# Expert stage of a routed MLP: transposes by DMA in place of TensorE, second product two tiles behind

## Chip, cores and metric

One of the eight cores of a Trainium2 chip runs the kernel. The metric is device time in microseconds from one launch, median of several runs; the profile's span reaches from the first to the last instruction of one profiled execution.

## What is computed

The input x is 8 x 512 rows of 512. A cross-attention layer over 120 context rows is added to x, and then an MLP in which each row goes through one of eight experts.

```python
x = x + xattn(ctx, ctx, layernorm(x), Wk, Wv, bv, Wq, bq, Wo, bo)     # scores, softmax, values, Wo
xf = layernorm(x)
idx = argmax(softmax(xf @ Wg + bg))                                   # one expert of 8 per row
h = gelu(xf @ W1[idx] + b1[idx])                                      # 512 -> 512
x = x + h @ W2[idx] + b2[idx]                                         # 512 -> 512
```

## The kernel before

The first part of the span computes attention for 32 tiles of 128 rows, the gate, and for each row its expert. GpSimd scatters each row (512 values, minus the mean, the inverse deviation, the row's number) to a buffer in HBM that is sorted by expert. A small table is then made, on the chip, of NJ = 39 tiles of 128 rows, each of one expert: its start row in the buffer and the offsets of its weights and biases.

The expert stage, which the change touches, takes these 39 tiles in turn. All weights lie in SBUF as two f16 halves (a high part, and a low part scaled by 64), which VectorE and ScalarE made in the first part (L571, L774). Per tile j:

- SP reads the start row (`first_row`, L376) and loads 128 rows (`load_rows`, L381), 258 KB, into one of R = 3 row buffers. It waits for `res_ready`, so until GpSimd has read the buffer that it overwrites.
- GpSimd normalizes the rows to the f32 tile xn2 (`xhat`, L508), copies the row ids (L515), adds b2 and the rows into a buffer of its own (`residual`, L516), and scatters the finished tile to the output (`send`, L521), two tiles behind. `residual` waits for the landing of an earlier scatter from the same buffer.
- TensorE transposes xn2 in four blocks of 128x128 f32 into a bank of PSUM (L1246). ScalarE copies the bank to f16, the high half (L696), and VectorE subtracts it from the bank for the low half (L986).
- TensorE makes the first product, `up`: eight matmuls with the high half of the rows against both halves of the weights (L1254), then four with the low half (L1258). VectorE adds b1 (`bias`, L981), ScalarE applies gelu in f32 (L702).
- TensorE transposes the gelu (L1270), ScalarE and VectorE split it as above (L707, L991), and TensorE makes the second product, `down` (again L1254, L1258). VectorE adds it to the residual (`finish`, L997).

The order on each engine is written by hand. In TensorE's stream one step is:

```python
up(j, ex)
transpose_x2(j + 1)
down(j - 1, ex_before)
transpose_g(j)
```

Six such steps are one turn of a loop, at whose head TensorE loads seven weight offsets into registers (`experts`). Before the stage TensorE waits until all weights are split (`low_done`).

## Time and profile before

| | us |
|---|---|
| runs | 511.59, 511.91, 509.14 |
| median | 511.59 |
| span of the profiled execution | 495.3 |
| expert stage, first product to end of span | 257.8 |

The profiled execution's own time is not listed apart from the runs; the median is 16.3 us above its span. The stage's first product starts at 237.53 us.

How to read it: the page gives the busy time of each engine over the span, and the span in 40 slices of 12.4 us, in which each digit is a busy share in tenths. The expert stage begins in the twentieth slice. The chain of waits goes back from the last instruction to what released it, and so names what sets the end; its pieces carry start and length. The views by windows and by line give how much each engine has to do in a stretch and how long one instruction takes.

### The profile page before, as it was taken

To read this page: it belongs to the slowest core of one execution; us is meant where nothing else is said; L and a number is where in the kernel's file an instruction comes from. 1 tells how busy PE (TensorE), PEld (TensorE's weight loads), DVE (VectorE), ACT (ScalarE), POOL (GpSimd) and SP (SyncE) were. 2 spreads that over 40 slices of the span, in tenths; PEclk is the share of its full clock that TensorE was granted. 3 is DMA by queue.
4 is the path that set the end of the run, shared out by engine and by line. 5 is a ranking of instruction groups with operands and counts; after the bars stand their busy time and mean duration, and the time that the engine had idled before them with its cause. 6 is when DMAs were issued, how large, how long until landed. Compare 5 with 4: busy or idle time off the path is not lost.

```text
span 495.3 us, 9245 instructions
## 1 busy us (share of the span) xinstructions
PE 436.0 (88%) x2362; PEld 257.4 (52%) x2363; DVE 258.2 (52%) x604; ACT 200.7 (41%) x411; POOL 189.8 (38%) x274
## 2 busy tenths in 40 slices
PE   6758999997999999920699999999999999999991
PEld 2355565565777676610355555555555555555540
DVE  0246999674577677767244444444444444434440
ACT  1142366547788887652122222222222222222220
POOL 7000002300054545453245545545545545545530
PEclk9969999999999999975799999999999999999996
DMA  8999985905356555684522222322222222222200
GB/s 254 309 314 384 376 280 209 369 2 207 121 155 203 166 174 171 180 328 145 183 79 88 71 78 81 88 81 79 91 71 85 85 84 85 70 85 74 65 2 0
DMA packets 33850, 73.97 MB, mean 149 GB/s; under 512 B 4376, under 2 KB 4388, under 8 KB 33575
## 3 DMA queue, kind: packets, MB, share of 16 engines
q1 hardware_dynamic: 26591, 54.22, 34.5%
q0 software_dynamic: 6400, 19.23, 10.2%
q10 hardware_dynamic: 840, 0.29, 0.4%
q8 instruction: 9, 0.15, 0.1%
q14 instruction: 10, 0.08, 0.1%
HBM read 54.50 MB, written 21.06 MB: 153 GB/s over the span
## 4 chain that ended last, share of the span: by engine, by line
PE 81%; DMA 5%; DVE 3%; issue 3%; POOL 2%; SPq 1%; ACT 1%; POOLq 0%; DVEq 0%; ACTq 0%
PE bank L1254 28%; PE bank L1258 14%; PE bank L1198 5%; PE bank L1180 5%; DMA work<-in_ctx 5%; PE bank L1160 4%; PE bank L1110 4%; PE bank L1270 3%; PE bank L1246 3%; PE bank L1088 3%; PE bank L1173 3%; PE bank L1191 1%; PE bank L1070 1%; PE bank L1183 1%; PE bank L1139 1%
## 5 line engine op out<-in xcount | busy, mean ns | idle before, releaser
L1254 PE MATMUL bank<-expert_weights,work 128*128 x624 | 149.2, 382 | 7.5 <-issue 5.8
L1254 PEld LDWEIGHTS bank<-expert_weights,work 128*128 128x128 f16 x624 | 61.3, 98 | 66.2 <-issue 11.3
L1258 PE MATMUL bank<-expert_weights,work 128*128 x312 | 80.5, 381 | 0.0
L696 ACT ACTIVATE work<-bank 128x512 f16<-128x512 f32 x39 | 23.3, 597 | 102.6 <-PE bank L1246 102.6
L981 DVE SCALAR_TENSOR_TENSOR work<-bank,keys_then_b 128x512 f32<-128x512 f32 x39 | 27.0, 692 | 64.1 <-PE bank L1258 64.1
L571 ACT ACTIVATE expert_weights<-expert_weights 128x512 f16<-128x512 f32 (+1 forms) x64 | 38.7, 626 | 40.2 <-DVE expert_weights L774 39.4
L997 DVE SCALAR_TENSOR_TENSOR work<-bank,work 128x512 f32<-128x512 f32 x39 | 27.0, 692 | 52.9 <-PE bank L1258 52.9
L707 ACT ACTIVATE work<-bank 128x512 f16<-128x512 f32 x39 | 23.3, 597 | 69.7 <-PE bank L1270 69.7
L521 POOL DMA_INDIRECT out_x<-work,output_ids x39 | 40.1, 1028 | 26.5 <-DVE work L997 18.7
L1258 PEld LDWEIGHTS bank<-expert_weights,work 128*128 128x128 f16 x312 | 30.7, 98 | 37.5 <-issue 1.1
L516 POOL TENSOR_TENSOR work<-work,values_then_b 128x512 f32<-128x512 f32 x39 | 49.1, 1258 | 0.0
L473 POOL DMA_INDIRECT routed_rows<-work,slot_index x32 | 32.3, 1010 | 35.4 <-DVE slot_index L868 28.1
L515 POOL COPY output_ids<-work 128x1 int32<-128x1 int32 x39 | 6.9, 178 | 99.4 <-DMA out_x<-work,output_ids 89.4
L774 DVE SCALAR_TENSOR_TENSOR expert_weights<-expert_weights 128x512 f16<-128x512 f32 (+1 forms) x64 | 41.7, 686 | 1.6 <-ACT expert_weights L571 1.2
L744 DVE BATCH_NORM_STATS2 stats<-expert_weights 128x6 f32<-128x512 f32 x32 | 20.5, 682 | 32.8 <-DMA expert_weights<-in_x 32.8
L986 DVE TENSOR_TENSOR work<-bank,work 128x512 f16<-128x512 f32 x39 | 27.0, 692 | 17.8 <-ACT work L696 17.8
L1198 PE MATMUL bank<-values_then_b,work 120*128 (+1 forms) x64 | 35.3, 634 | 0.0
L1246 PE MATMUL bank<-identity,work 128*128 128x128 f32 x156 | 23.9, 277 | 11.5 <-POOL work L508 11.5
L1180 PE MATMUL bank<-keys_then_b,work 128*128 (+1 forms) x256 | 33.8, 275 | 0.0
L508 POOL TENSOR_SCALAR work<-work 128x512 f32<-128x512 f32 x39 | 29.6, 759 | 7.5 <-DMA work<-routed_rows 6.0
L991 DVE TENSOR_TENSOR work<-bank,work 128x512 f16<-128x512 f32 x39 | 27.0, 692 | 9.7 <-ACT work L707 9.7
L1180 PEld LDWEIGHTS bank<-keys_then_b,work 128*128 128x128 f32 x256 | 31.2, 192 | 0.5 <-issue 0.5
(154 smaller groups left out, 613.6 us busy)
## 6 DMA issues: line engine op xcount, KB each, us to landing
expert_weights<-in_L_ffn_W SPq DMA_DIRECT2D x14, 1024.0 KB, 9.3
work<-routed_rows SPq DMA_DIRECT2D x39, 258.0 KB, 2.7
expert_weights<-in_x SPq DMA_DIRECT2D x16, 512.0 KB, 8.7
expert_weights<-in_x SPq DMA_DIRECT2D x32, 256.0 KB, 3.0
routed_rows<-values_then_b POOLq DMA_DIRECT2D x9, 258.0 KB, 9.3
expert_weights<-in_L_ffn_W SPq DMA_DIRECT2D x8, 256.0 KB, 3.1
keys_then_b<-in_L_ffn_b SPq DMA_DIRECT2D x1, 2048.0 KB, 7.8
values_then_b<-in_L_ffn_b SPq DMA_DIRECT2D x1, 2048.0 KB, 10.5
```

Of the source, the lines that this page charges most:

```text
L473: pool.indirect_dma_start(routed, bass.IndirectOffsetOnAxis(ap=slot_i[:, j:j + 1], axis=0), rows[:, j, :], None).then_inc(sent[j], 16)
L508: nc.gpsimd.tensor_scalar(xn2, rrow[r][:, 0:D], rrow[r][:, D:D + 1], rrow[r][:, D + 1:D + 2], ALU.add, ALU.mult).then_inc(xn2_ready, 1)
L516: nc.gpsimd.tensor_tensor(res[r], rrow[r][:, 0:D], vals[:, bass.ds(ex, D)], ALU.add).then_inc(res_ready, 1)
L521: pool.indirect_dma_start(out_rows, bass.IndirectOffsetOnAxis(ap=out_id[:, r:r + 1], axis=0), res[r], None, bounds_check=T - 1, oob_is_err ...
L571: nc.scalar.activation(w_split[:, bass.ds(n * 2 * D, D)], wall[:, bass.ds((n + GAP) * D, D)], ACT.Copy, scale=WSCALE).then_inc(high_done, 1)
L774: nc.vector.scalar_tensor_tensor(w_split[:, bass.ds(n * 2 * D + D, D)], wall[:, bass.ds((n + GAP) * D, D)], WSCALE, w_split[:, bass.ds(n * ...
L981: nc.vector.scalar_tensor_tensor(hid, bank[1][:, :], 1.0 / WSCALE, keys[:, bass.ds(ex, D)], ALU.mult, ALU.add).then_inc(hb_done, 1)
L1180: mm(bank[2 + j % 2][:, 0:P], xnT[j % 2][:, c, :], keys[:, bass.ds((b * C + c) * P, P)], start=(c == 0), stop=False)
L1198: mm(bank[6 + j % 2][:, :], probT[j % 2], vals[0:K, bass.ds(b * D, D)], start=True, stop=True)\
L1246: last = nc.tensor.transpose(bank[0][:, P * c:P * (c + 1)], xn2[:, P * c:P * (c + 1)], ident[:, :])
L1254: mm(o, a[:, 0, c, :], w_split[:, bass.ds(first + (2 * c + h) * D, D)], start=(c == 0 and h == 0), stop=False)
L1258: last = mm(o, a[:, 1, c, :], w_split[:, bass.ds(first + 2 * c * D, D)], start=False, stop=(c == C - 1))
```

## The change

It takes all transposes of the expert stage from TensorE. xn2 and the gelu are split into f16 halves in their natural layout, by ScalarE and VectorE from SBUF; the two halves of a tile stand side by side, 128 rows of 1024 f16, and one DMA transpose, issued by SP, brings them into eight blocks of 128x128 for the products. There are two such DMAs in a tile, each with two buffers in turn.

The second product of a tile now comes two tiles behind its first. GpSimd adds b2 and VectorE adds the product in place in the row buffer, from which the scatter goes out; there are eight row buffers, and SP loads a tile four ahead once the scatter of eight tiles before has landed. SP starts with the transposes after all weights are split. All engines step through the tiles in loops of eight, and TensorE loads ten weight offsets per turn.

```diff
-R = 3
-NJTURN = NJ // R
+R = 8
+LAG = 2
+FIRST = 3
+NJTURN = (NJ - FIRST) // R
...
         rrow = [carve(ROW) for _ in range(R)]
-        res = [carve(D) for _ in range(R)]
-        xn2, x2T, hid, gel, gelT = (carve(D) for _ in range(5))
-        ge = carve(NJ * E).rearrange("p (j e) -> p j e", j=NJ)
-        tv = carve(4 * NJ).rearrange("p (v j) -> p v j", v=4)
+        xn2, hid, g0, g1 = (carve(D) for _ in range(4))
         assert at[0] <= U * ROW + 4 * D
-
-        x2T = x2T.bitcast(F16).rearrange("p (h c t) -> p h c t", h=2, c=C)
-        gelT = gelT.bitcast(F16).rearrange("p (h c t) -> p h c t", h=2, c=C)
-        out_id = sb("output_ids", [P, R], I32)
-
+        gel_split = [g.bitcast(F16) for g in (g0, g1)]
+        xn2_split = [split_area[:, n, :] for n in range(2)]
+        x2T = [w_split[:, E * NW * 2 * D + 2 * D * n:E * NW * 2 * D + 2 * D * (n + 1)].rearrange("p (k t) -> p k t", t=P)
+               for n in range(2)]
+        gelT = [bias_area[:, D * n:D * (n + 1)].bitcast(F16).rearrange("p (k t) -> p k t", t=P) for n in range(2)]
+        ge = g1[:, 0:NJ * E].rearrange("p (j e) -> p j e", j=NJ)
+        tv = g1[:, NJ * E:NJ * E + 4 * NJ].rearrange("p (v j) -> p v j", v=4)
...
+        def each_step(eng, step, first, end):
+
+            for n in range(first, FIRST):
+                step(Slot(n))
...
-            def load_rows(j, r, start):
-
-                sp.wait_ge(res_ready, j + 1)
-                sp.dma_start(rrow[r], routed[bass.ds(start, P), :]).then_inc(row_in[r], 16)
-
-            starts = [first_row(r) for r in range(R)]
+            def load_rows(t, start):
+
+                wait_apart(sp, out_sent[t.buf], 16 * t.turn, sp_waits)
+                sp.dma_start(rrow[t.buf], routed[bass.ds(start, P), :]).then_inc(row_in[t.buf], 16)
+
+            starts = [first_row(n) for n in range(3)]
...
+            sp.wait_ge(tabled, 3)
+            for n in range(3):
+                load_rows(Slot(n), starts[n])
...
-            with sp.Fori(1, NJTURN) as i:
-                for r in range(R):
-                    load_rows(i * R + r, r, first_row(i * R + r))
+            sp.wait_ge(low_done, E * NW)
+
+            def transpose_x2(t):
+                wait_apart(sp, x2l_done, t.j + 1, sp_waits)
+                wait_apart(sp, h_done, t.j - 1, sp_waits)
+                sp.dma_start_transpose(x2T[t.half], xn2_split[t.half]).then_inc(x2T_in[t.half], 16)
+
+            def transpose_g(t):
+                wait_apart(sp, gl_done, t.j + 1, sp_waits)
+                wait_apart(sp, y_done, t.j - 1, sp_waits)
+                sp.dma_start_transpose(gelT[t.half], gel_split[t.half]).then_inc(gT_in[t.half], 16)
+
+            def step(t):
+                if (t + 1).real:
+                    transpose_x2(t + 1)
+                if (t + 4).real:
+                    load_rows(t + 4, first_row((t + 4).j))
+                if (t - 1).real:
+                    transpose_g(t - 1)
+
+            each_step(sp, step, -1, NJ + 1)
...
+            def xhat(t):
+                wait_apart(pool, row_in[t.buf], 16 * t.turn + 16, pool_waits)
+
+                wait_apart(pool, x2l_done, t.j, pool_waits)
+                nc.gpsimd.tensor_scalar(xn2, rrow[t.buf][:, 0:D], rrow[t.buf][:, D:D + 1], rrow[t.buf][:, D + 1:D + 2],
                                         ALU.add, ALU.mult).then_inc(xn2_ready, 1)
...
+            def residual(t):
+
+                ex = pool.value_load(table[0:1, 2, bass.ds(t.j, 1)], min_val=0, max_val=(E - 1) * D)
+                nc.gpsimd.tensor_tensor(rrow[t.buf][:, 0:D], rrow[t.buf][:, 0:D], vals[:, bass.ds(ex, D)],
                                         ALU.add).then_inc(res_ready, 1)
 
-            def send(j, r):
-                wait_apart(pool, out_done, j + 1, pool_waits)
-                pool.indirect_dma_start(out_rows, bass.IndirectOffsetOnAxis(ap=out_id[:, r:r + 1], axis=0),
-                                        res[r], None, bounds_check=T - 1, oob_is_err=False).then_inc(out_sent[r], 16)
-
-            xhat(0, 0, 0)
-            xhat(1, 1, 0)
+            def send(t):
+                wait_apart(pool, out_done, t.j + 1, pool_waits)
+                ids_of = bass.IndirectOffsetOnAxis(ap=rrow[t.buf][:, D + 2:D + 3].bitcast(I32), axis=0)
+                pool.indirect_dma_start(out_rows, ids_of, rrow[t.buf][:, 0:D], None, bounds_check=T - 1,
+                                        oob_is_err=False).then_inc(out_sent[t.buf], 16)
...
+            def step(t):
+                if (t + 2).real:
+                    xhat(t + 2)
+                if t.real:
+                    residual(t)
+                if (t - 3).real:
+                    send(t - 3)
+
+            each_step(pool, step, 0, NJ + 3)
...
+            def x2_high(t):
+                act.wait_ge(xn2_ready, t.j + 1)
+                need(act, x2T_in[t.half], 16 * t.pair)
+                nc.scalar.activation(xn2_split[t.half][:, 0:D], xn2, ACT.Copy).then_inc(x2h_done, 1)
+
+            def gelu(t):
+                act.wait_ge(hb_done, t.j + 1)
+                nc.scalar.activation(hid, hid, ACT.Gelu).then_inc(g_done, 1)
+
+            def g_high(t):
+                act.wait_ge(g_done, t.j + 1)
+                need(act, gT_in[t.half], 16 * t.pair)
+                nc.scalar.activation(gel_split[t.half][:, 0:D], hid, ACT.Copy).then_inc(gh_done, 1)
+
+            def step(t):
+                if (t + 2).real:
+                    x2_high(t + 2)
+                if t.real:
+                    gelu(t)
+                    g_high(t)
+
+            each_step(act, step, -2, NJ)
...
+            def bias(t):
+                ex = dve.value_load(table[0:1, 2, bass.ds(t.j, 1)], min_val=0, max_val=(E - 1) * D)
+                dve.wait_ge(h_done, t.j + 1)
+                need(dve, gl_done, t.j)
+                nc.vector.scalar_tensor_tensor(hid, bank[t.half][:, :], 1.0 / WSCALE, keys[:, bass.ds(ex, D)], ALU.mult,
                                                ALU.add).then_inc(hb_done, 1)
 
-            def x2T_low(j):
-                dve.wait_ge(x2h_done, j + 1)
-                nc.vector.tensor_tensor(x2T[:, 1, :, :], bank[0][:, :].rearrange("p (c t) -> p c t", c=C),
-                                        x2T[:, 0, :, :], ALU.subtract).then_inc(x2l_done, 1)
-
-            def gT_low(j):
-                dve.wait_ge(gh_done, j + 1)
-                nc.vector.tensor_tensor(gelT[:, 1, :, :], bank[2][:, :].rearrange("p (c t) -> p c t", c=C),
-                                        gelT[:, 0, :, :], ALU.subtract).then_inc(gl_done, 1)
-
-            def finish(j, r):
-                dve.wait_ge(y_done, j + 1)
-                dve.wait_ge(res_ready, j + 1 + R)
-                nc.vector.scalar_tensor_tensor(res[r], bank[3][:, :], 1.0 / WSCALE, res[r], ALU.mult,
-                                               ALU.add).then_inc(out_done, 1)
-
-            def step(j, r):
-                if not isinstance(j, int) or j + 1 < NJ:
-                    bias(j + 1)
-                if not isinstance(j, int) or j + 2 < NJ:
-                    x2T_low(j + 2)
-                finish(j, r)
-                if not isinstance(j, int) or j + 1 < NJ:
-                    gT_low(j + 1)
-
-            x2T_low(0)
-            bias(0)
-            x2T_low(1)
-            gT_low(0)
-            with dve.Fori(0, NJTURN - 1) as i:
-                for r in range(R):
-                    step(i * R + r, r)
-            for r in range(R):
-                step(NJ - R + r, r)
+            def x2_low(t):
+                dve.wait_ge(x2h_done, t.j + 1)
+                nc.vector.tensor_tensor(xn2_split[t.half][:, D:2 * D], xn2, xn2_split[t.half][:, 0:D],
+                                        ALU.subtract).then_inc(x2l_done, 1)
+
+            def g_low(t):
+                dve.wait_ge(gh_done, t.j + 1)
+                nc.vector.tensor_tensor(gel_split[t.half][:, D:2 * D], hid, gel_split[t.half][:, 0:D],
+                                        ALU.subtract).then_inc(gl_done, 1)
+
+            def finish(t):
+                dve.wait_ge(y_done, t.j + 1)
+                dve.wait_ge(res_ready, t.j + 1)
+                nc.vector.scalar_tensor_tensor(rrow[t.buf][:, 0:D], bank[2 + t.half][:, :], 1.0 / WSCALE,
+                                               rrow[t.buf][:, 0:D], ALU.mult, ALU.add).then_inc(out_done, 1)
+
+            def step(t):
+                if (t - 3).real:
+                    finish(t - 3)
+                if (t - 1).real:
+                    g_low(t - 1)
+                if (t + 2).real:
+                    x2_low(t + 2)
+                if t.real:
+                    bias(t)
+
+            each_step(dve, step, -2, NJ + 3)
...
-            def product(o, a, first, low_ready, j):
-
+            def product(o, a, first):
 
                 for c in range(C):
                     for h in range(2):
-                        mm(o, a[:, 0, c, :], w_split[:, bass.ds(first + (2 * c + h) * D, D)],
+                        mm(o, a[:, c, :], w_split[:, bass.ds(first + (2 * c + h) * D, D)],
                            start=(c == 0 and h == 0), stop=False)
-                pe.wait_ge(low_ready, j + 1)
                 for c in range(C):
-                    last = mm(o, a[:, 1, c, :], w_split[:, bass.ds(first + 2 * c * D, D)], start=False, stop=(c == C - 1))
+                    last = mm(o, a[:, C + c, :], w_split[:, bass.ds(first + 2 * c * D, D)], start=False, stop=(c == C - 1))
...
+            def up(t, ex):
+                pe.wait_ge(x2T_in[t.half], 16 * t.pair + 16)
+                need(pe, hb_done, t.j - 1)
+                product(bank[t.half][:, :], x2T[t.half], ex).then_inc(h_done, 1)
+
+            def down(t, ex):
+                pe.wait_ge(gT_in[t.half], 16 * t.pair + 16)
+                need(pe, out_done, t.j - 1)
+                product(bank[2 + t.half][:, :], gelT[t.half], ex + C * 2 * D).then_inc(y_done, 1)
...
+            def steps(first, n):
+                ex = experts(first.j, n + LAG)
+                for q in range(n):
+                    t = first + LAG + q
+                    if t.real:
+                        up(t, ex[q + LAG])
+                    down(t - LAG, ex[q])
+
+            ex = experts(0, LAG)
+            for n in range(LAG):
+                up(Slot(n), ex[n])
+            steps(Slot(0), FIRST - LAG)
+            with pe.Fori(0, NJTURN) as i:
+                steps(Slot(FIRST - LAG, i), R)
+            last = FIRST - LAG + R * NJTURN
+            steps(Slot(last), NJ - LAG - last)
+            ex = experts(NJ - LAG, LAG)
+            for n in range(LAG):
+                down(Slot(NJ - LAG + n), ex[n])
```

## Rows read from the trace of the kernel before

**Rows 1.** the page: busy time, then tenths in 40 slices of clock and DMA

```profile
PE 436.0 (88%) x2362; PEld 257.4 (52%) x2363; DVE 258.2 (52%) x604; ACT 200.7 (41%) x411; POOL 189.8 (38%) x274
...
PEclk9969999999999999975799999999999999999996
DMA  8999985905356555684522222322222222222200
```

**Rows 2.** the chain of waits from 382 us: start us, us, what

```profile
382.18 0.44 PE bank L1270 x4
382.62 1.73 PE bank L1254 x8
384.34 0.86 PE bank L1258 x4
...
394.72 0.80 issue
395.53 1.90 PE bank L1254 x8
```

**Rows 3.** busy us of each engine in a window of six tiles

```profile
core 0: us, PE busy (x) PEld busy (x) DVE busy (x) ACT busy (x) POOL busy (x), PEclk, DMA share, GB/s
283.59:320.90 37.31, 36.50 (x193) 19.73 (x193) 16.54 (x25) 10.28 (x18) 19.10 (x25) 1.00 0.27 83
```

**Rows 4.** who waited for whom, 250 to 480 us: total, times, longest

```profile
POOL output_ids L515 <- DMA out_x<-work,output_ids: 89.4, 35, 2.7
```

**Rows 5.** by line, 250 to 480 us: line, engine, shapes, count, busy, mean ns

```profile
L516 POOL TENSOR_TENSOR work<-work,values_then_b 128x512 f32<-128x512 f32 x36 | 45.3, 1258 | 0.0
L521 POOL DMA_INDIRECT out_x<-work,output_ids x37 | 38.2, 1032 | 18.9 <-DVE work L997 11.1 <-issue 7.8
...
L508 POOL TENSOR_SCALAR work<-work 128x512 f32<-128x512 f32 x36 | 27.3, 758 | 0.8 <-DMA work<-routed_rows 0.8
...
L991 DVE TENSOR_TENSOR work<-bank,work 128x512 f16<-128x512 f32 x37 | 25.6, 692 | 9.1 <-ACT work L707 9.1
L702 ACT ACTIVATE work<-work 128x512 f32<-128x512 f32 x38 | 23.6, 622 | 2.8 <-DVE work L981 2.8
...
L707 ACT ACTIVATE work<-bank 128x512 f16<-128x512 f32 x37 | 22.1, 597 | 67.8 <-PE bank L1270 67.8
```

**Rows 6.** the page's groups that split weights out of SBUF

```profile
L571 ACT ACTIVATE expert_weights<-expert_weights 128x512 f16<-128x512 f32 (+1 forms) x64 | 38.7, 626 | 40.2 <-DVE expert_weights L774 39.4
...
L774 DVE SCALAR_TENSOR_TENSOR expert_weights<-expert_weights 128x512 f16<-128x512 f32 (+1 forms) x64 | 41.7, 686 | 1.6 <-ACT expert_weights L571 1.2
```

**Rows 7.** one line's instructions: SP's register load and row load; landing of the scatter

```profile
L376 SPq FUSED_REGOPS  x63: 37/152/170, 229.8 to 452.4; - x63
L376 SPq TENSOR_LOAD <-tile_table x39: 263/267/554, 229.3 to 452.1; - x39
...
L381 SPq DMA_DIRECT2D work<-routed_rows x39: 332/333/347, 231.9 to 457.7; - x39
...
DMA to landing us min/median/max: 2.5/2.7/4.4
...
DMA to landing us min/median/max: 2.1/2.8/2.9
```

**Rows 8.** the page: DMA queues

```profile
q1 hardware_dynamic: 26591, 54.22, 34.5%
...
q10 hardware_dynamic: 840, 0.29, 0.4%
```

**Rows 9.** the timeline at the stage's start: start us, us, instruction

```profile
234.50 0.76 POOL L508 TENSOR_SCALAR work<-work 128x512 f32<-128x512 f32 x1 [5.18 <-DMA work<-routed_rows]
...
237.53 3.59 PE L1254 MATMUL bank<-expert_weights,work 128*128 x8 [0.93 <-ACT work L696]
240.92 1.46 PE L1258 MATMUL bank<-expert_weights,work 128*128 x4
```

**Rows 10.** the chain of waits at the end: TensorE's last product

```profile
483.70 0.88 PE bank L1258 x4
```

158 lines of the change are left out of this document (46 added, 112 removed).

## The prediction

> **What bounds the kernel now.** [...] Eight matmuls take 1.73 us, the four with the low half 0.86 us, four transposes 0.44 us, and then the next product starts; the only break is 0.80 us of "issue" when the register loads for six tiles come [rows 2]. So one tile costs 2 x (1.73 + 0.86 + 0.44) = 6.06 us of TensorE, and the stage by its windows 37.31 us for six tiles, or 6.22 us with the register loads [rows 3]. No other engine comes near this: VectorE has 2.8 us of work in a tile, ScalarE 1.7 us, GpSimd 3.2 us, and GpSimd's waits are for the landing of its own scatter and end in time [rows 3 to 5]. TensorE is the bound, and 0.88 us of each 6.22 are transposes.
>
> **What is removed.** 2 x 4 transposes in each of 39 tiles: 39 x 0.88 = 34.3 us, all of it on the chain [rows 2]. A product without them costs 1.73 + 0.86 = 2.59 us, a tile 5.18 us. The register loads stay: 0.80 us before for seven values per six tiles; now ten values per eight tiles, between 0.80 and 0.80 x 10/7 = 1.14 us, so 1.0; 5.18 + 1.0/8 = 5.30 us per tile is the new floor. Also removed: the 0.18 us copy of row ids on GpSimd and its wait for the scatter (89.4 us in total), which cost nothing, since GpSimd was not late [rows 4].
>
> **What is only exchanged.** ScalarE's two copies to f16 now read SBUF instead of PSUM: 0.63 us in the nearest row, 0.60 before [rows 5, 6]. VectorE's two subtractions likewise: 0.69 in both [rows 5, 6]. These rows are both of whole 128x512 tiles, so the bounds are 0.03 us apart and TensorE hides them. VectorE keeps 4 x 0.69 = 2.8 us, ScalarE 0.62 + 2 x 0.63 = 1.9, GpSimd 0.76 + 1.26 + 1.03 = 3.05 us, all under 5.30 [rows 5, 6].
>
> **What is added: two DMA transposes per tile on SP.** Each moves 128 rows of 1024 f16, 256 KB, SBUF to SBUF; no row of the trace shows such an instruction. It has three prices.
>
> First, SP's own time, I. The lower bound is the plain issue of a transfer of the same size on the same engine, 0.33 us [rows 7]. That row cuts its transfer into 128 pieces; a transpose in blocks of 128 elements has 8 x 128 = 1024 pieces of 256 bytes. At the plain rate (0.33/128 = 2.6 ns a piece) that is 2.7 us; at the rate of GpSimd's scatter (1.03 us for 128 rows) it is 8.2 us [rows 5, 7]. I take 1.0 us, nearer to the plain row, because it is the same engine and a regular pattern; the range keeps the others. SP needs besides, in a tile, 0.33 us for the row load, and 0.27 + 0.15 us for its start row; with the waits I take 0.9 us [rows 7]. SP is hidden while 2I + 0.9 < 5.30, that is I < 2.2 us, and costs more than is gained from 2I + 0.9 > 6.22, I > 2.7 us.
>
> Second, the DMA engines. They are busy 27% of 37.31 us for six tiles, 1.68 us a tile for two transfers of 256 KB [rows 3]. With two more at that rate 3.4 us a tile: hidden. The hardware queue's mean packet costs 0.345 x 495.3 x 16 / 26591 = 103 ns for 2 KB, the small packets of queue 10 cost 38 ns for 345 bytes [rows 1, 8]; if each of 1024 pieces costs 38 ns, a transpose keeps the 16 engines 2.4 us and a tile 1.68 + 4.9 = 6.5 us. I take the lower one, since packet times hold latency that overlaps.
>
> Third, the latency, from issue to landing, L. Row loads land in 2.5 to 4.4 us, 2.7 in the median [rows 7]. I take 4.0 us for the transposes. The x half of tile t may start when the product of tile t-2 has let go of its buffer, and TensorE has three other products in between, 7.8 us. The gelu half: after the first product of t, VectorE's bias, gelu, copy, then on VectorE the finish of tile t-2 (which waits 2.6 us for its product), then the low half: done 4.1 us after the first product [rows 5, 6]. The second product of t comes four products after it, 10.4 us, so the transpose has 6.3 us. Both hide L = 4.0 us. That is what "two tiles behind" is worth: with one tile behind there would be 5.2 us for a chain of at least 2.9 + 2.7.
>
> **Added waits, and what is queued behind them.** On SP stands in order: x transpose of t+1, row load of t+4 (waits for the scatter of t-4, which lands 2.1 to 2.9 us after its issue), gelu transpose of t-1 [rows 7]. The scatter is issued 0.85 us after its product ends, so it has landed 3.7 us after that, or 1.1 us after the next first product is done; the gelu transpose behind it is due only 4.1 us after. Cost nothing; if the landing took 3 us more, the cover would be gone and TensorE would wait for the rest. On VectorE the bias of t is queued behind the low half of x of t+2; that waits for GpSimd, which is done a period earlier.
>
> **Start and end, by the timeline.** [...] After: copy 0.63, subtraction 0.69, L = 4.0, first product at 240.7, 3.2 us later, ending at 245.5 with the same 4.85 us. Tile 1 follows until 248.1. The transpose of tile 2 waits for the first product, lands at 249.5, its product ends 252.1; the gelu chain of tile 0 (2.8 us) with its transpose is ready at 252.3. So at 254.9 us four of 78 products are done. The other 74 x 2.59 = 191.7 and 7 register loads of 1.0 give 453.6. At the end the last gelu comes 8.1 us after the last first product, two products cover 5.2, so 2.9 us of stall: 456.5 us. Before, TensorE ends at 484.6 [rows 10]. What follows is the same, so 28.1 us are gained of the span of 495.3, to 467.2. The 16.3 us between the span and the median of 511.6 I leave as they are: **483.5 us**. With L = 2.7 start and end lose some 3 us less, 480; with a floor of 2.59 us per product and no stall, 477.
>
> [...] In rows, four transposes of 128x128 cost TensorE 0.44 us, 0.11 each, where they stand between products [rows 2]. [...]
>
> **Rival 1 (slower): SP's issue time becomes the period.** [...] It decides from I = 2.2 us, and is a loss above 2.7. For it: 1024 pieces instead of 128, and 2.7 us is just what the plain rate gives; SP also has all three DMAs of a tile in line. Against: the plain 256 KB issue is 0.33 us and SP is nearly empty now [rows 7]. At I = 3.5 us (an estimate between 2.7 and 8.2, in the lower part) a tile takes 7.9 us: 39 x (7.9 - 6.22) + 6 for start and end = 72 us more, 583 us. At I = 2.2 to 2.7 it lies between 484 and 518.
>
> [...]
>
> **Rival 2 (slower): the DMA engines become the period.** [...] From a transpose that takes 2.7 times as long as a plain transfer, 1.68 + 2 x 0.84 x 2.7 = 6.2 us, the gain is gone. At the 6.5 us worked out above: 39 x 0.3 + 6 = 18 us more, 529 us. For it: the price of small packets [rows 8]. Against: three quarters of the DMA time is free [rows 3].
>
> **Rival 3 (part of the gain).** A period between 5.5 and 6.0 us, because rate, latency and the order on SP act together: 490 to 507 us.
>
> **How the numbers follow.** Forecast (TensorE stays the bound, 477 to 490 us): 0.48. Rival 3: 0.07. Within 0.5%, which is about what a measurement of this kernel can tell from no change: 0.04, from the two slower rivals near their break-even. Rival 1 slower: 0.26. Rival 2 slower: 0.15. So faster 0.55, same 0.04, slower 0.41. The range has to hold both signs: from 475 (forecast without stalls, less the spread of the runs) to 600 (I = 3.7 us); left out are the dear ends of the rivals. If TensorE stays the bound, its own range is 477 to 490 us.
>
> **What the profile of the changed kernel will show.** Right: the chain in mid-stage is matmuls alone, windows of eight tiles take 42.4 us, the granted clock stays at the upper level, SP's transposes take under 2.2 us each, first product at about 240.7. Rival 1: TensorE waits for the transposes, SP's transposes fill the period back to back. Rival 2: SP idle or waiting, DMA share near its limit, landing times over 6 us. If TensorE has gaps in every tile, its clock may also fall to the lower level, as it is before the stage's first product [rows 1, 9], and a product would take twice the time, which would make either slower rival dearer. Wrong in all cases: if GpSimd or VectorE ends the wait of the matmuls.

## The result

The kernel after takes 483.12 us (median of 4 runs, 481.99 to 487.42), the kernel before beside it 511.75 us (509.14 to 513.35): ratio 0.9474, 95% interval 0.9434 to 0.9514, 28.6 us less. The forecast was 483.5 us, with 28.1 us less.

The profiled execution took 481.99 us and has a span of 480.3 us. So 1.7 us lie around the span, not 16.3: the profile that stands ahead of the prediction is of an execution some 15 us quicker than the median given with it. Where those microseconds lie is the first experiment's matter.

The page of after: busy time, the tenths of TensorE's clock and of the DMA engines, packets, and the hardware queue.

```profile
PE 409.1 (85%) x2050; PEld 223.8 (47%) x2051; DVE 251.8 (52%) x604; ACT 203.5 (42%) x411; POOL 188.7 (39%) x235
...
PEclk9969999999999988998557899999999999999997
DMA  7999975913535454458476999989888987999720
...
DMA packets 116221, 94.46 MB, mean 197 GB/s; under 512 B 86744, under 2 KB 86756, under 8 KB 115943
...
q1 hardware_dynamic: 108959, 74.68, 60.9%
```

Against [rows 1] TensorE is 27 us less busy, VectorE 6 us less; ScalarE and GpSimd are within 3 us of what they were. The DMA engines, at two tenths in the right half before, stand at eight and nine tenths. There are 116221 packets instead of 33850.

The chain of waits from the middle of the stage: start us, us, what.

```profile
338.89 1.73 PE bank L1292 x8
340.61 0.86 PE bank L1295 x4
...
356.15 0.86 PE bank L1295 x4
357.02 0.09 issue
357.11 1.90 PE bank L1292 x8
```

This is [rows 2] without its 0.44 us rows: a tile is 2 x (1.73 + 0.86) = 5.18 us, and at the loop head "issue" is 0.09 us instead of 0.80. A window of one loop turn, which is 8 tiles (window; busy us of PE, PEld, DVE, ACT, POOL; clock; DMA share; GB/s):

```profile
315.41:357.11 41.70, 41.61 (x193) 18.80 (x193) 20.35 (x33) 14.24 (x24) 25.40 (x24) 1.00 0.90 196
```

41.70 us for 8 tiles are 5.21 us a tile, where [rows 3] had 6.22. TensorE is still the bound, at the upper level of its clock (1.00 in this window). The DMA share is 0.90 instead of 0.27, that is 4.7 us of DMA time in a tile of 5.2. The transposes on SP, one line each for the x half and the gelu half (min/median/max ns), and the time from issue to landing of the gelu half and of the output scatter:

```profile
L450 SPq DMA_TRANSPOSE expert_weights<-key_bias_split_then_xn x39: 1231/1307/3336, 248.9 to 449.4; - x39
...
L455 SPq DMA_TRANSPOSE key_bias_then_geluT<-work x39: 746/1272/1599, 263.1 to 463.6; - x39
```

```profile
DMA to landing us min/median/max: 2.8/4.2/6.2
...
DMA to landing us min/median/max: 2.1/4.2/5.9
```

(The first landing row is of the same kernel in the run e5_after_again below.) A transpose keeps SP 1.3 us in the median, and that of the gelu half lands 4.2 us after its issue. The scatter's landing rose from 2.8 to 4.2 us [rows 7].

The start of the stage, by the chain of waits:

```profile
243.86 2.57 DMA work<-routed_rows
...
247.41 0.64 ACT key_bias_split_then_xn L754
...
248.17 0.70 DVE key_bias_split_then_xn L1039
...
248.94 6.94 DMA expert_weights<-key_bias_split_then_xn
...
256.01 1.03 PE bank L1292 x2
```

The first transpose needs 6.94 us to land. Ahead of it in the queue stands b2, 2 MB, issued at 245.31.

### The profile page after: what moved, and what is told of

It is laid out like the page before. It is cut to its first block, busy times and chain, and to the rows that moved or that the text cites. A ratio compares the mean times of both kernels' runs of the same rounds, so it can differ in the third digit from the quotient of the medians.

```text
span 480.3 us, 8534 instructions
## 1 busy us (share of the span) xinstructions
PE 409.1 (85%) x2050; PEld 223.8 (47%) x2051; DVE 251.8 (52%) x604; ACT 203.5 (42%) x411; POOL 188.7 (39%) x235
## 2 busy tenths in 40 slices
DMA packets 116221, 94.46 MB, mean 197 GB/s; under 512 B 86744, under 2 KB 86756, under 8 KB 115943
## 3 DMA queue, kind: packets, MB, share of 16 engines
q0 software_dynamic: 6400, 19.23, 11.1%
## 4 chain that ended last, share of the span: by engine, by line
PE 66%; DMA 11%; issue 5%; DVE 5%; SPq 4%; ACT 3%; POOL 2%; another core or an unknown queue 1%; ACTq 0%; DVEq 0%; POOLq 0%
PE bank L1292 24%; PE bank L1295 12%; DMA work<-in_ctx 5%; PE bank L1206 4%; PE bank L1226 4%; PE bank L1156 4%; PE bank L1244 4%; PE bank L1134 3%; PE bank L1219 3%; DMA key_bias_then_geluT<-work 3%; PE bank L1237 2%; PE bank L1116 1%; DMA expert_weights<-key_bias_split_then_xn 1%; ACT work L687 1%; SPq L450 1%
## 5 line engine op out<-in xcount | busy, mean ns | idle before, releaser
L1292 PE MATMUL bank<-expert_weights 128*128 x312 | 75.1, 384 | 22.2 <-DMA expert_weights<-key_bias_split_then_xn 20.8
L758 ACT ACTIVATE work<-work 128x512 f32<-128x512 f32 x39 | 24.6, 631 | 135.8 <-DVE work L1034 135.8
L589 POOL DMA_INDIRECT out_x<-work x39 | 45.3, 1162 | 87.2 <-DVE work L1050 85.0
L1292 PE MATMUL bank<-expert_weights,key_bias_then_geluT 128*128 x312 | 74.7, 383 | 4.5 <-DMA key_bias_then_geluT<-work 4.5
L1292 PEld LDWEIGHTS bank<-expert_weights 128*128 128x128 f16 x312 | 30.9, 99 | 60.8 <-issue 26.9
L1292 PEld LDWEIGHTS bank<-expert_weights,key_bias_then_geluT 128*128 128x128 f16 x312 | 30.7, 98 | 42.5 <-issue 7.7
L1295 PE MATMUL bank<-expert_weights,key_bias_then_geluT 128*128 x156 | 40.8, 385 | 0.0
L1295 PE MATMUL bank<-expert_weights 128*128 x156 | 40.0, 379 | 0.0
L1244 PE MATMUL bank<-values_then_b,work 120*128 (+1 forms) x64 | 37.3, 665 | 0.0
L797 DVE BATCH_NORM_STATS2 stats<-expert_weights 128x6 f32<-128x512 f32 x32 | 20.5, 682 | 31.5 <-DMA expert_weights<-in_x 31.4
L1226 PE MATMUL bank<-keys_then_b,work 128*128 (+1 forms) x256 | 35.1, 282 | 0.1
L1039 DVE TENSOR_TENSOR key_bias_split_then_xn<-work,key_bias_split_then_xn 128x512 f16<-128x512 f32 x39 | 27.0, 692 | 10.3 <-ACT key_bias_split_then_xn L754 10.3
L1044 DVE TENSOR_TENSOR work<-work 128x512 f16<-128x512 f32 x39 | 26.6, 682 | 2.7 <-ACT work L763 2.7
```

The costliest lines, as they stand in the source:

```text
L589: pool.indirect_dma_start(out_rows, ids_of, rrow[t.buf][:, 0:D], None, bounds_check=T - 1, oob_is_err=False).then_inc(out_sent[t.buf], 16)
L1039: nc.vector.tensor_tensor(xn2_split[t.half][:, D:2 * D], xn2, xn2_split[t.half][:, 0:D], ALU.subtract).then_inc(x2l_done, 1)
L1226: mm(bank[2 + j % 2][:, 0:P], xnT[j % 2][:, c, :], keys[:, bass.ds((b * C + c) * P, P)], start=(c == 0), stop=False)
L1244: mm(bank[6 + j % 2][:, :], probT[j % 2], vals[0:K, bass.ds(b * D, D)], start=True, stop=True)\
L1292: mm(o, a[:, c, :], w_split[:, bass.ds(first + (2 * c + h) * D, D)], start=(c == 0 and h == 0), stop=False)
L1295: last = mm(o, a[:, C + c, :], w_split[:, bass.ds(first + 2 * c * D, D)], start=False, stop=(c == C - 1))
```

## Experiments

The kernel before ran beside each of them: 498.83 us in the median beside e1 to e4, 499.30 beside e5 to e8, 499.74 beside e9 to e11, 12 to 13 us less than in the result above. Each ratio below is against the runs of before beside it. "After" means the changed kernel.

**1. The two kernels again (e1_before_again, e5_after_again).** No edit. The table of tiles was ready at 229.15 us in the profile of before and at 241.09 us in that of after, in a part that the change hardly touches. Either that is the change's doing and the stage gained 12 us more than it seems, or it belongs to the execution.

> The kernel before, unchanged, for a second profile. In the first profile of before the first product of the expert stage starts at 237.5 us and the span is 495.3; in that of after it starts at 256.0 us, of which some 12 us arose before the stage, in attention tiles whose code is the same. Theory A: these 12 us come and go with the program's execution and have nothing to do with the change; then this profile may show the first product near 249.5 us and a span of 507 to 510 us, which fits the timed runs of 509 to 513 us. Theory B: the change itself lengthened the first part; then 237.5 and 495 us again, and the timed runs of before stay 16 us above the span.

> The changed kernel, unchanged, beside the next three on one chip. Theory A (the 12 us by which its first profile was later before the expert stage belong to that chip, where before took 511.7 us too, and not to the change): on a chip where before takes 499 us the tile table is ready at 229 to 231 us, as in before, the first product starts at 244 to 246 us, and the ratio to before is 0.945 to 0.95 as in the first measurement. Theory B (the change itself lengthens the first part by 12 us): the table is ready at 241 us again and the ratio is 0.97.

Before: 499.76 us (498.25 to 502.19), table at 230.2 us. After: 471.77 us (469.65 to 472.04), table at 229.9 us, ratio 0.945 (0.9419 to 0.948). The first run alone decides nothing: its times lie at 499.8 us and not at 509 to 513, so what its two theories were to tell apart did not occur. The second does: table and ratio come as its theory A says. So the 12 us do not belong to the change. In the first measurement both kernels had them, here neither has them. Both kernels have 1.7 us around the span, so the prediction's "16.3 us around the span" was a slower attention part. In the first profile of after the delay arises between 145 and 218 us. Its chain of waits has three stalls there, of 1.23, 1.78 and 1.86 us, that the profile puts down to "another core or an unknown queue", and that of e5_after_again has none. That is 4.9 us; what these stalls are, and the rest, is open.

This pair has the same start and is the balance sheet for the stage. TensorE's timeline at the first and the last product, before and then after:

```profile
238.69 3.59 PE L1254 MATMUL bank<-expert_weights,work 128*128 x8 [0.93 <-ACT work L696]
...
487.68 1.03 PE L1258 MATMUL bank<-expert_weights,work 128*128 x4
```

```profile
245.53 3.59 PE L1292 MATMUL bank<-expert_weights 128*128 x8 [20.72 <-DMA expert_weights<-key_bias_split_then_xn]
...
253.65 1.90 PE L1292 MATMUL bank<-expert_weights 128*128 x8 [0.77 <-DMA expert_weights<-key_bias_split_then_xn]
...
256.95 1.90 PE L1292 MATMUL bank<-expert_weights,key_bias_then_geluT 128*128 x8 [0.54 <-DMA key_bias_then_geluT<-work]
...
455.82 1.90 PE L1292 MATMUL bank<-expert_weights,key_bias_then_geluT 128*128 x8 [1.87 <-DMA key_bias_then_geluT<-work]
457.56 1.03 PE L1295 MATMUL bank<-expert_weights,key_bias_then_geluT 128*128 x4
```

The first product starts 6.8 us later (245.53 against 238.69). From there to the last product's end it takes 213.1 us instead of 250.0, 37.0 us less. The rest of the span is equal to 0.1 us (10.7 and 10.8). Net: 30.0 us of the span (499.4 to 469.4), where the medians of the two runs differ by 28.0. This execution of before is a dear one: its clock was at the lower level (granted clock 0.50) for 6.8 us of the stage, from 246.5 to 253.3. The execution ahead of the prediction was at the upper level there (1.00), and its stage took 247.1 us (237.53 to 484.58). Against that one the stage gained 34.0 us.

**2. One tile behind instead of two (e3_lag1).**

```diff
-LAG = 2
+LAG = 1
```

> The changed kernel with the second product one tile behind in place of two. Theory A (the second tile of lag hides the gelu's chain): that chain takes 2.9 us until the low half is done and 3.3 to 4.5 us for its transpose, 6.2 to 7.5 us in all, TensorE has 5.2 us of other work in between, so a tile takes (6.2 to 7.5 + 5.2)/2 = 5.7 to 6.3 us in place of 5.2, and the kernel 503 to 526 us. Theory B (the latency is hidden by one tile too): 483 us as before.

535.91 us (534.31 to 541.52), ratio 1.0734 (1.0692 to 1.0776): slower than before. Its window in mid-stage, and its waits there (who waited, for what: total us, times, longest):

```profile
285.00:495.00 210.00, 164.24 (x699) 70.78 (x700) 76.13 (x118) 52.25 (x89) 100.58 (x88) 0.95 0.66 143
```

```profile
PE bank L1292 <- DMA key_bias_then_geluT<-work: 41.7, 17, 3.5
```

699 matmuls are 29.1 tiles of 24, so 7.2 us a tile, dearer than the forecast. TensorE waits for the gelu's transpose in 17 of them, 41.7 us, and the clock, 1.00 in after, is 0.95 here: a part of the products ran at the lower level (eight matmuls at 381.03 us took 3.51 us, at a granted clock of 0.52). The kind of the loss was foreseen; its size, with the clock, was not.

**3. Six row buffers (e10_six_buffers).**

```diff
-R = 8
+R = 6
...
-NJTURN = (NJ - FIRST) // R
+NJTURN = (NJ - FIRST) // R - 1
```

> The changed kernel with six row buffers instead of eight; the row load of tile t+4 then waits for the scatter of tile t-2 instead of t-4, and the gelu's transpose of t-1 is queued behind it on SP. Theory A (a wait at the head of SP's queue holds the transposes behind it): the scatter of t-2 lands 5.1 us after its product, then 0.4 us for the load, 3 to 4.5 us for the transpose, and only then the next second product: 11 to 13 us a tile in place of 5.2, more if the clock falls, so 700 to 800 us. Theory B (the eight buffers are only room; the wait is covered by the lag): under 500 us.

746.13 us (746.12 to 746.15), ratio 1.4943 (1.4855 to 1.503). The load of the rows of tile t + 4 now waits on SP for the scatter of t - 2, and so for its second product; behind it stand the gelu transpose of t - 1 and the x transpose of t + 2. The second product of t - 1 can be prepared only when that of t - 2 has been scattered. Its window, and the timeline of one tile:

```profile
300.00:600.00 300.00, 156.85 (x529) 61.35 (x528) 56.81 (x88) 41.56 (x66) 70.50 (x66) 0.75 0.33 75
```

```profile
401.61 0.36 SPq L432 DMA_DIRECT2D work<-routed_rows  x1
402.17 1.28 SPq L455 DMA_TRANSPOSE key_bias_then_geluT<-work  x1
403.64 1.27 SPq L450 DMA_TRANSPOSE expert_weights<-key_bias_split_then_xn  x1
...
405.67 3.59 PE L1292 MATMUL bank<-expert_weights,key_bias_then_geluT 128*128 x8 [6.28 <-DMA key_bias_then_geluT<-work]
```

A tile takes 13.6 us (529 matmuls in 300 us). The row load at 401.61, which had waited for a scatter, lets both transposes go within 2 us, and TensorE has stood for 6.28 us. In all, SP waits 193 of the 300 us for the landing of a scatter, 22 times. Its clock is 0.75, and after such a wait eight matmuls take 3.59 us, twice 1.73. The forecast of 700 to 800 us held. What is cheap in the change hangs on the number of buffers: a wait at the head of SP's queue holds both transposes back.

**4. The x half back on TensorE (e6_x_half_on_tensor).** The x transposes stand on TensorE again, behind the product of two tiles ahead; the gelu goes by DMA as in after. The core of the edit:

```diff
             def step(t):
-                if (t + 1).real:
-                    transpose_x2(t + 1)
...
+            def transpose_x2(t):
+                pe.wait_ge(xn2_ready, t.j + 1)
+                need(pe, x2l_done, t.j - 1)
+                for c in range(C):
+                    last = nc.tensor.transpose(bank[4 + t.half][:, P * c:P * (c + 1)], xn2[:, P * c:P * (c + 1)], ident[:, :])
```

> Half of the change undone: xn2 is again transposed by TensorE (four transposes a tile, into two banks in turn) and split from the bank; only the gelu goes by DMA. Theory A (TensorE is the bound, a set of four transposes costs 0.44 us of it): 39 x 0.44 = 17 us slower in the stage, some 6 us faster at the start, where the transpose's landing is not waited for, so 10 to 12 us slower than the changed kernel. DMA share in mid-stage falls from 0.90 to 0.60. Theory B (the DMA engines or SP are what sets the changed kernel's pace): not slower, or faster.

474.91 us (474.44 to 476.18), ratio 0.9524 (0.9486 to 0.9562), 3.1 us more than after, measured beside it. The same window of after and then of this kernel:

```profile
260.00:428.00 168.00, 164.21 (x757) 73.96 (x756) 81.68 (x127) 55.62 (x94) 99.34 (x94) 1.00 0.93 193
```

```profile
260.00:428.00 168.00, 168.00 (x840) 84.19 (x839) 76.98 (x121) 52.40 (x90) 90.75 (x90) 1.00 0.52 137
```

Here TensorE is busy in all 168.00 us, 5.6 us a tile; in after it stands idle for 3.8 us of them. From the first product to the last one's end it takes 223.9 us, 10.9 more than after; the 39 x 0.44 = 17.2 us come in full, but some 6 us of waits for transposes are gone, which after has. The first product comes at 238.47, 7.1 us earlier. So theory A has the direction and not the size: it did not count those waits, and its 10 to 12 us became 3.1.

The x half by DMA is worth 3.1 us. This kernel gains 24.4 us against before with one transpose by DMA only, but not all of that is the gelu's transpose. The stage is 223.9 us instead of 247.1 (experiment 1), 23.2 us less; the gelu's transposes are 17.2 us of them. The other 6 come with the rest of the edit: the order of the products, the buffers, the register loads. No run takes these apart.

**5. More traffic (e8_more_dma).** Two loads of 192 KB a tile that nobody reads:

```diff
+                    for n in range(2):
+                        wait_apart(sp, spare_in[n], 16 * ((t + 4).j - 3), sp_waits)
+                        sp.dma_start(spare[n][:, :], x_rows[0:P, 0:384]).then_inc(spare_in[n], 16)
```

> The changed kernel with two more plain loads a tile on SP, 192 KB each, into memory that nothing reads. Theory A (the DMA engines are next to bound, 4.7 us a tile of 5.2): 0.75 x 0.84 = 0.63 us of their time each, 4.7 + 1.26 = 6.0 us a tile, the kernel 25 to 35 us slower, DMA share near 1. Theory B (SP's issue time is next, some 3.9 us a tile, and the DMA share counts overlapping latency): SP rises to 3.9 + 0.9 = 4.8 us, still under 5.2, and the time moves by less than 5 us.

492.83 us (490.99 to 494.07), ratio 0.9886 (0.9846 to 0.9927), 21 us more than after.

```profile
260.00:428.00 168.00, 153.60 (x686) 67.21 (x685) 73.55 (x115) 50.68 (x85) 88.74 (x84) 0.99 1.02 241
```

```profile
PE bank L1297 <- DMA key_bias_then_geluT<-work: 14.1, 19, 2.2
```

686 matmuls: 28.6 tiles of 5.9 us, at a DMA share of 1.02, and TensorE waits for the gelu's transpose in 19 of them. What sets this pace is read from the chain of waits in mid-stage, which is SP's own work (here from 320 to 345 us, shares by line), and from SP's timeline (L434 the row load, L466 the two loads added, L457 and L452 the transposes; the register load L429 stands between L452 and L434):

```profile
by line: SPq L452 28.6%; SPq L457 26.1%; issue 15.6%; SPq L429 13.2%; SPq L466 11.6%; SPq L434 6.9%; SPq L56 2.1%; SPq L55 0.6%
```

```profile
341.34 0.36 SPq L434 DMA_DIRECT2D work<-routed_rows  x1
341.89 0.84 SPq L466 DMA_DIRECT2D spare<-in_x  x2
342.92 1.27 SPq L457 DMA_TRANSPOSE key_bias_then_geluT<-work  x1
344.37 1.77 SPq L452 DMA_TRANSPOSE expert_weights<-key_bias_split_then_xn  x1
347.34 0.37 SPq L434 DMA_DIRECT2D work<-routed_rows  x1
```

SP goes from one instruction to the next, 6.0 us for this tile, and in the whole window the profile has not one wait of SP. So SP is the bound here. In after (e5_after_again), in the same window, SP waits 7.0 us, 6.7 of them for scatters:

```profile
SPq L56 <- DMA out_x<-work: 6.7, 5, 1.8
```

That leaves 161.0 us of SP's time for 31.5 tiles, 5.1 us a tile, beside TensorE's 5.18. The two added loads bring it to 5.9. Theory B named the right engine and took 3.9 us for what is 5.1. The DMA share went from 0.93 to 1.02 (5.0 to 6.0 us a tile). It adds up the times of the packets, and over 1.00 some of them must overlap, so it does not say how much more the DMA engines can carry. No run shows them as the bound.

**6. Less TensorE work (e4_two_thirds, e11_half_width).** Both leave out the four matmuls of each product that use the low half of the activations, so their output is not the reference's. e11_half_width also transposes the high half alone, 512 columns instead of 1024 (below, for the gelu; the x half likewise).

```diff
-                for c in range(C):
-                    last = mm(o, a[:, C + c, :], w_split[:, bass.ds(first + 2 * c * D, D)], start=False, stop=(c == C - 1))
...
-                sp.dma_start_transpose(gelT[t.half], gel_split[t.half]).then_inc(gT_in[t.half], 16)
+                sp.dma_start_transpose(gelT[t.half][:, 0:C, :], gel_split[t.half][:, 0:D]).then_inc(gT_in[t.half], 16)
```

> The changed kernel with 8 of 12 matmuls in each product: the four with the low half of the activations are left out (the low half is still made and transposed). TensorE then needs 3.45 us a tile, so what comes next shows. Theory A (DMA engines next: share 0.90 of 5.2 us, 4.7 us a tile): windows of eight tiles 38 us, kernel 463 to 470 us. Theory B (SP next, 1.3 + 1.3 + 0.4 + 0.6 + waits, 3.9 us a tile): 432 to 440 us. Theory C (neither near): 3.5 us a tile, 415 to 420 us.

> The kernel with 8 of 12 matmuls in a product, and now both transposes move only the high half, 512 columns in place of 1024 (the low halves are made but not transposed and not used). With full width it ran at 4.7 us a tile with the DMA share at 0.9, TensorE needing 3.45. Theory A (the DMA engines' time for the transposes set that pace, 1.5 us each): their time falls to 1.7 + 2 x 0.75 = 3.2 us a tile, the period to 3.5 to 3.9 us, 31 to 47 us less than the 447.5 measured with full width, 400 to 417 us. Theory B (a latency or the fixed part of SP's work set it): less than 15 us faster.

447.5 us (447.33 to 449.4), ratio 0.8983 (0.8949 to 0.9018); and 430.77 us (430.27 to 431.05), ratio 0.8627 (0.8586 to 0.8668). The windows, in this order:

```profile
270.00:420.00 150.00, 114.25 (x502) 48.96 (x503) 79.13 (x124) 57.78 (x94) 99.10 (x94) 1.00 0.92 211
```

```profile
270.00:396.00 126.00, 102.68 (x455) 44.17 (x454) 74.09 (x115) 50.20 (x85) 90.04 (x86) 1.00 0.68 171
```

With 16 matmuls a tile TensorE needs 4 x 0.86 = 3.45 us. The first has 31.4 tiles of 4.8 us at a DMA share of 0.92, the second 28.4 tiles of 4.4 us at 0.68. The chain of waits from 320 to 345 us is SP's again, in both kernels (L455 and L450 the transposes, L427 the register load, L432 the row load):

```profile
by line: SPq L455 30.6%; SPq L450 24.6%; SPq L427 19.3%; issue 16.0%; SPq L432 8.5%; SPq L56 1.7%; SPq L55 1.0%; SPq L350 0.6%
```

```profile
by line: SPq L455 29.5%; SPq L450 28.6%; issue 18.7%; SPq L427 15.4%; SPq L432 10.3%; SPq L56 1.9%; SPq L55 1.0%; SPq L350 0.6%
```

SP waits 0.6 us in the 150 us of the first window and 0.7 us in the 126 us of the second. So the next limit behind TensorE is SP, at 4.8 us a tile here: theory B of e4_two_thirds by its engine, though it put SP at 3.9 us; the 447.5 us lie between what its theories A and B gave. With half the columns, 0.92 x 4.8 = 4.4 us of DMA time a tile became 0.68 x 4.4 = 3.0 us, yet the period fell by 0.4 us only and the kernel by 16.7 us. That is the fixed part of SP's work, theory B of e11_half_width, a little more than its 15 us. The 0.4 us are SP's: its register load (L427) takes 0.42 us in the median instead of 0.73, each transpose 0.04 us less. SP's time for a transpose hardly fell with the columns (e11_half_width):

```profile
L450 SPq DMA_TRANSPOSE expert_weights<-key_bias_split_then_xn x39: 1188/1189/1350, 236.8 to 404.3; - x39
```

**7. The load of b2 ahead of the row loads (e2_b2_early).**

```diff
+            sp.wait_ge(pad_out, 16 * (E + 1))
+            sp.wait_ge(pv_done, NT)
+            sp.dma_start(vals[:, :], b2.rearrange("e d -> (e d)").partition_broadcast(P)).then_inc(b2_in, 16)
             sp.wait_ge(tabled, 1)
...
-            sp.wait_ge(pv_done, NT)
-            sp.dma_start(vals[:, :], b2.rearrange("e d -> (e d)").partition_broadcast(P)).then_inc(b2_in, 16)
             sp.wait_ge(low_done, E * NW)
```

> The changed kernel with the load of b2 (2 MB) issued before SP waits for the tile table, not between the first row loads and the first transpose. In the changed kernel the first transpose is issued at 248.9 us and lands at 255.9, 7 us later, behind b2's packets. Theory A (the transpose waited behind b2 on the DMA engines): it lands in 3 to 4 us, the first product starts 3 to 4 us earlier, and the kernel takes 479 to 480 us, 3 to 4 less. Theory B (a transpose from SBUF to SBUF takes 7 us by itself when the pipeline is cold): the time stays at 483 us.

467.2 us (465.14 to 468.74), ratio 0.9367 (0.9335 to 0.9399); after had 0.945, so by the ratios this is 4.1 us less, and theory A holds. The chain of waits:

```profile
238.47 3.21 DMA expert_weights<-key_bias_split_then_xn
...
241.81 3.59 PE bank L1293 x8
```

The first transpose lands after 3.21 us instead of 6.94 (7.41 in e5_after_again), and the first product starts at 241.81, 3.1 us after that of before. The other half of the loss at the start was the 2 MB load ahead of it. Whether it is the place in the queue or the shared DMA engines, the run does not tell. That 3.1 us meets the prediction's 3.2 is partly luck: the landing took 0.8 us less than the 4.0 put in, and gaps between the steps and a later first row made up for it.

**8. The low half of the gelu ahead of the finish (e7_low_half_first).** e2_b2_early with VectorE's two steps exchanged:

```diff
-                if (t - 3).real:
-                    finish(t - 3)
                 if (t - 1).real:
                     g_low(t - 1)
+                if (t - 3).real:
+                    finish(t - 3)
```

> The kernel with the early load of b2, and on VectorE the low half of the gelu of tile t-1 before the finish of tile t-3 instead of behind it. Theory A: the gelu's transpose is issued 1.2 us earlier; at the end the stall of 1.8 us before the last product shrinks to 0.6 and the short stalls in mid-stage (0.4 to 1 us in a window of 42) get fewer: 1 to 2 us less than with the early load alone. Theory B (it delays the finish and so the scatter and the row load): same or 1 us more.

464.47 us (464.09 to 467.57), ratio 0.9319 (0.9286 to 0.9353), some 2.4 us less than e2_b2_early by the ratios, but the two intervals overlap. TensorE's last product, with its wait:

```profile
452.00 1.90 PE L1293 MATMUL bank<-expert_weights,key_bias_then_geluT 128*128 x8 [0.58 <-DMA key_bias_then_geluT<-work]
```

The wait ahead of the last product is 0.58 us; it was 1.87 in after and 1.68 in e2_b2_early. From the first product to the last one's end it takes 212.1 us instead of 212.9. So 0.8 to 1.1 us are shown, at the end of the stage, not 2.4.

**9. The first tile by TensorE (e9_first_tile_on_tensor).** e7_low_half_first, but the x half of tile 0 is transposed by TensorE, which is idle there, and split out of the bank.

```diff
+            pe.wait_ge(xn2_ready, 1)
+            for c in range(C):
+                last = nc.tensor.transpose(bank[4][:, P * c:P * (c + 1)], xn2[:, P * c:P * (c + 1)], ident[:, :])
+            last.then_inc(tx2_done, 1)
```

> On top of the early load of b2 and the low half before the finish: the x half of tile 0 alone is transposed by TensorE, which is idle then anyway, and split from the bank; all other transposes stay DMAs. Theory A (the first product waits for the landing of one DMA transpose, 3.2 us and more): the first product starts at 238.5 us instead of 241.8 to 242.6, tile 1's DMA lands while it runs, and the kernel takes 460 to 462 us, 3 to 4 less than with the two edits, where before takes 499. Theory B (the pipeline's fill is set by what follows, b2, the gelu's chain): same as with the two edits, 464.5.

464.53 us (463.58 to 466.0), ratio 0.9302 (0.9267 to 0.9338), no measurable difference from e7_low_half_first. The timeline of TensorE:

```profile
238.55 3.59 PE L1307 MATMUL bank<-expert_weights 128*128 x8 [1.67 <-DVE expert_weights L1051]
...
249.24 1.90 PE L1307 MATMUL bank<-expert_weights 128*128 x8 [2.40 <-DMA expert_weights<-key_bias_split_then_xn]
```

The first product starts at 238.55, as forecast, and that is 4.1 us earlier than in the profile of e7_low_half_first. But there the table of tiles was ready 2.2 us later; counted from the table, the edit gains 1.9 us. Then the third product waits 2.40 us for its transpose, which landed 5.3 us after its issue. From the first product to the last one's end it takes 213.8 us instead of 212.1, so 1.7 of the 1.9 us are given back: theory B holds for the total. e7_low_half_first and this one are the fastest of those that compute the whole result, 7 us ahead of after.

## Why the prediction came out right

**TensorE stays the bound, at 5.30 us a tile.** Right, and for the reason given: the chain is matmuls alone, 1.73 and 0.86 us, and a loop turn of 8 tiles takes 41.7 to 42.2 us where 42.4 were forecast. 16 products are 41.4 us, so all else, the register loads among it, costs 0.3 to 0.8 us a turn, where 1.0 was taken for the register loads alone. Why they cost less than the 0.80 us of [rows 2] no run shows.

**SP's issue time, I = 1.0 us with the break-even at 2.2.** It is 1.3 us in the median, and rival 1 did not come, but by far less than the prediction saw. The term it had wrong is what SP does besides: it took 0.9 us for the row load, the start row and the waits. By experiment 5 SP needs 5.1 us a tile, so the rest is 5.1 - 2 x 1.3 = 2.5 us: the register load has doubled (0.63 us), the steps between the instructions add up, and single transposes take up to 3.3 us. With 2.5 us besides, the break-even lies at I = 1.3 us, which is where I is. Rival 1 failed by 0.1 us of 5.2. The pieces were the wrong scale: I worked out 2.7 us at the plain rate for 1024 pieces, and with half the columns (e11_half_width, 544 packets for each transpose instead of 1056) SP's time stays at 1.2 us, 0.04 us less at the least (1188 against 1231 ns). Between these two sizes it is nearly a fixed price.

**The DMA engines, 3.4 us a tile.** Mis-sized. There are (116221 - 33850)/78 = 1056 packets for each transpose, so the 1024 pieces were right. In the hardware queue they cost (0.609 x 480.3 - 0.345 x 495.3) us x 16 / 82371 = 23.6 ns each, less than the 38 ns of [rows 8] but more than the plain rate by bytes: 1056 x 23.6 ns / 16 = 1.56 us of all engines, not 0.84. The tile stands at 4.7 to 5.0 us of DMA time, where the prediction saw three quarters of the DMA time free. It moved nothing: rival 2 did not come in any run, and even at a share of 1.02 SP was the bound. The reason for the lower value, that packet times hold latency that overlaps, is right in kind: the share of 1.02 in e8_more_dma cannot be without overlap, and in the same queue packets of 2 KB take 103 ns [rows 8] and those of the transposes, of 256 bytes, 23.6 ns, so for 8 times the bytes 4.4 times the time: a part of it does not grow with the bytes. As a reason for 0.84 us it was too weak. How near the DMA engines themselves are to their limit stays open.

**The latency, L = 4.0 us, hidden by "two tiles behind".** Right. The median is 4.2 us, and with one tile behind, experiment 2, the change is a loss of 7%. After still has some 6 us of waits for transposes behind its first product, 5.2 of them for the gelu half, at the stage's two ends and at four places between. The longest between, 1.25 us at 295.96 in e5_after_again, is SP's doing. The chain of waits goes back from it over a landing of 6.73 us to SP's instructions, end to end from 262 us on, one of them a transpose of 3.04 us:

```profile
272.71 3.04 SPq L455
...
289.10 6.73 DMA key_bias_then_geluT<-work
...
295.96 1.25 PE bank L1292 x5
```

**Waits on SP cost nothing.** Nearly so with eight buffers, and experiment 3 shows what the wrong number costs. The cover is thinner than forecast: the scatter's landing rose to 4.2 us in the median. SP waits for one five times in the window of experiment 5, 1.8 us at the longest, and one of these waits (for a scatter that took 5.12 us) reaches TensorE as 0.33 us at 322.36.

**The start, first product 3.2 us later.** It is 6.8 us later. The step that failed is L at this place: 7 us instead of 4, behind the 2 MB of b2. I had listed what each transpose waits for, but not what is ahead of it in the DMA queue. Experiment 7 moves that load and finds 3.1 us, partly by luck as said there. The sum starts from xn2(0), ready at 235.27 us, and gives the first product the 4.85 us that it takes in before [rows 9], at a granted clock of 0.56 instead of 1.00.

**The end, 2.9 us of stall.** 1.9 us in the pair of experiment 1.

The sum, between the first product's start and the last one's end in experiment 1, without 39 x 5.18 = 202.0 us: forecast 13.8 us (lower clock in the first product 2.3, stalls of the start 1.6, register loads 7.0, end 2.9). Measured 11.1 us: 2.3, 1.3, register loads 1.0, end 1.9, and 2.8 of waits for the gelu in mid-stage that the forecast did not have; 1.8 are left over, gaps too small to name. So 2.7 us less here and 3.6 us more at the start: the errors all but cancel, and 28.1 against 28.6 us is nearer than the steps were. The largest of them is the register loads, 7.0 us forecast and 1.0 measured. That is luck in the number; the mechanism, that TensorE stays the bound without its transposes, held by a margin of 0.1 us a tile that the prediction did not know of.

One sum in the prediction does not come out: 477 us as the lower end "with a floor of 2.59 us per product and no stall". Without the 7.0 us of register loads it is 476.5, and without the 4.5 us of stalls too it is 472.

**The fixed part, 16.3 us.** Wrong, as experiment 1 shows; it moved nothing, because the slower attention part is in both kernels.

## What to carry to other kernels

A transpose can be taken off a full TensorE by DMA if the product that uses it runs far enough behind and nothing on the issuing queue waits for that product: here two tiles behind gained 5.5% (e5_after_again) and one tile behind lost 7% (e3_lag1), and with six buffers, where the queue waits, the kernel took 746 us (e10_six_buffers). Add up all that the issuing engine does in a tile, with its register loads and the steps between: here 5.1 us of 5.2, almost half of it not transposes. A rising DMA share is not yet the bound: even at 1.02 it was SP (e8_more_dma); ask the chain of waits, and whether the issuing engine ever waits. Do not count the DMA time by bytes alone: here 256 KB in 1056 packets cost 1.56 us of all engines where a plain transfer of that size costs 0.84, and the share went from 0.27 to 0.90. For each DMA at the start of a stage look at what stands ahead of it in its queue, and put what is big and not urgent elsewhere: the first transpose landed after 6.94 and 7.41 us behind 2 MB, and after 3.21 us with that load moved ahead (e2_b2_early). A span that lies 16 us below the median is a question to ask before using either.

## What the hardware showed

- A DMA transpose of 128 rows of f16 keeps SP 1.2 to 1.3 us in the median, with 1024 columns (after, e5_after_again) and with 512 (e11_half_width). Single ones took up to 3.3 us in after and 3.6 us in e5_after_again, there while the 2 MB load was under way.
- Two such transposes, a row load and a register load keep SP 5.1 us a tile in after; with less TensorE work SP sets the pace, at 4.8 us (e4_two_thirds), and at 4.4 us with 512 columns (e11_half_width).
- With 1024 columns a transpose is 1056 packets of 23.6 ns in the mean, and its gelu half lands in 2.8 to 6.2 us, 4.2 in the median, beside other traffic (e5_after_again). With 512 columns the gelu half lands in 2.9 us in the median (e11_half_width). In the time of the DMA engines the one with 1024 columns goes at about half the rate of the plain transfers of the same size (1.56 us against 0.84).
- SP's load of a register from the tile table takes 634 ns in the median beside the transposes (after), 416 beside those of 512 columns (e11_half_width), 267 before [rows 7].
- Both kernels took 12 us more in the first measurement (511.75 and 483.12 us) than in the three later ones (499.76 and 471.77 in experiment 1), ahead of the expert stage. The cause is open.
